# Deformable convolution: half blocks that share partitions, a map convolution read from SBUF, contraction in 32x32 tiles

## What is computed

```python
offset = conv2d(x, offset_w, offset_b)            # 3x3, 18 channels: (dy, dx) of 9 taps
mask = sigmoid(conv2d(x, mask_w, mask_b))         # 3x3, 9 channels
py = hs + ky + dy                                 # one sampling position per pixel and tap
px = ws + kx + dx
val = bilinear gather of x at (py, px), zero outside the image      # b k h w c
out = einsum('bkhwc,bkhw,ock->bohw', val, mask, weight)
x = x + out
```

## Time and profile before

| | us |
|---|---|
| median of 3 runs | 2114.85 |
| lowest and highest | 2094.2 and 2151.25 |
| profiled execution | 2127.27 |
| its span, first to last instruction | 2125.5 |
| PE busy | 1895.2 (89%) |
| DVE busy | 1278.3 (60%) |
| ACT busy | 1128.9 (53%) |
| POOL busy | 789.2 (37%) |

### The profile page before, as it was taken

The page is one execution under the profiler, slowest core; times in us unless marked ns, Lnnn a source line. Parts: engine busy times, 40 slices in busy tenths (PEclk is TensorE's granted clock), DMA queues, the critical chain, the costliest instruction groups (busy, mean ns, idle before and its releaser), DMA issues. The chain is left out here.

```text
span 2125.5 us, 58757 instructions
## 1 busy us (share of the span) xinstructions
PE 1895.2 (89%) x21269; PEld 1344.1 (63%) x21269; DVE 1278.3 (60%) x2688; ACT 1128.9 (53%) x3617; POOL 789.2 (37%) x743
## 2 busy tenths in 40 slices
PE   5599999999999998389999999596949999999998
PEld 3466666666666665145555556395827787778876
DVE  5178888888888888258878878642372222222222
ACT  2378888888888887357777778200211111111111
POOL 0077878878787876133323333000000011001100
PEclk9989999999999999589999999855879999999999
DMA  4400000000000000566666665240022111221110
GB/s 165 134 20 28 28 27 23 27 26 28 23 28 26 28 24 23 142 169 186 190 185 191 181 175 143 59 71 11 11 55 51 40 36 36 52 56 36 36 36 15
DMA packets 164173, 150.01 MB, mean 71 GB/s; under 512 B 60070, under 2 KB 151340, under 8 KB 163935
## 3 DMA queue, kind: packets, MB, share of 16 engines
q1 hardware_dynamic: 164014, 147.88, 26.2%
HBM read 83.18 MB, written 45.89 MB: 61 GB/s over the span
## 5 line engine op out<-in xcount | busy, mean ns | idle before, releaser
L412 ACT ACTIVATE at_probs<-at_sc,at_nmx 128x196 f32<-128x196 f32 x1152 | 473.0, 423 | 114.2 <-DVE at_nmx L358 114.2
L340 POOL TENSOR_TENSOR at_probs<-at_probs,at_rs 128x784 f32<-128x784 f32 x288 | 429.9, 1493 | 152.9 <-DVE at_rs L363 152.8
L358 DVE TENSOR_REDUCE at_nmx<-at_sc 128x4 f32<-128x784 f32 x288 | 277.4, 963 | 122.3 <-PE at_sc L436 122.3
L447 PE MATMUL at_pt<-at_ident,at_probs 128*98 128x128 f32 x2304 | 311.1, 278 | 40.6 <-DVE at_pts L368 40.0
L447 PEld LDWEIGHTS at_pt<-at_ident,at_probs 128*98 128x98 f32 x2304 | 241.1, 128 | 141.2 <-POOL at_probs L340 78.8
L436 PE MATMUL at_sc<-at_kw,at_qw 32*128 32x196 f32 x2304 | 272.1, 355 | 12.0 <-POOL at_qw L329 8.1
L1247 ACT ACTIVATE dn_mix<-dn_mps 128x432 f32<-128x432 f32 x384 | 182.3, 528 | 114.1 <-PE dn_mps L1142 110.6
L1930 POOL TENSOR_TENSOR fc_spo<-fc_prod 128x256 f32<-128x256 f32 x72 | 52.2, 725 | 502.6 <-DVE fc_prod L1974 502.6
L2031 PE MATMUL fc_qps<-fc_wk,fc_xs 99*128 99x128 f32 x1728 | 208.4, 278 | 31.3 <-DMA fc_xs<-in_ones 31.3
L412 ACT ACTIVATION_READ_ACCUMULATOR at_probs<-at_sc,at_nmx 128x1 f32 x1152 | 235.9, 205 | 0.0
L2031 PEld LDWEIGHTS fc_qps<-fc_wk,fc_xs 99*128 99x128 f32 x1728 | 202.0, 194 | 42.0 <-issue 39.1
(11 more groups left out here) (155 smaller groups left out, 2527.9 us busy)
## 6 DMA issues: line engine op xcount, KB each, us to landing
fc_xs<-fc_xp SPq DMA_DIRECT2D x144, 120.0 KB
dn_slab<-near_image SPq DMA_DIRECT2D x72, 200.0 KB, 4.2
at_vs<-attention_values SPq DMA_DIRECT2D x288, 49.0 KB
dn_offs<-near_maps SPq DMA_DIRECT2D x24, 486.0 KB
near_corners<-dn_split SPq DMA_DIRECT2D x24, 486.0 KB
dn_stack<-near_corners SPq DMA_DIRECT2D x24, 486.0 KB
dn_patch<-near_pixels SPq DMA_DIRECT2D x24, 384.0 KB
attention_values<-ap_vrow SPq DMA_DIRECT2D x21, 256.0 KB, 2.3
```

The lines of the kernel that those rows point to most:

```text
L340: nc.gpsimd.tensor_tensor(probs[s][p][:, :, :, :], probs[s][p][:, :, :, :], rs[s][:, 2 * p:2 * p + 2, :].unsqueeze(3).broadcast_to([P, 2, ...
L358: nc.vector.tensor_reduce(nmx[s][:, 2 * p:2 * p + 2, :], sc[p][:, :, 0:2 * NK].rearrange("p b (j k) -> p b j k", j=2), AX.X, ALU.max, nega ...
L412: nc.scalar.activation(probs[s][p][:, b, j, :], sc[p][:, b, NK * j:NK * j + NK], ACT.Exp, bias=nmx[s][:, 2 * p + b, j:j + 1], accum_out=su ...
L447: mm = nc.tensor.transpose(pt[b % 2][0:HK, o:o + P], probs[s][p][:, b % 2, j, HK * c:HK * c + HK], ident[:, :])
```

## The change

A block is now two half blocks of HBW = 4 columns each, 48 blocks of pixels being replaced by NBLK = 12 blocks of 8 columns. A half block reaches (4+4) x (4+4) = 64 pixels, so that the two halves lie in partitions 0 to 63 and 64 to 127 of `patch` and `mix`, and one column of the moving operand serves two output pixels. A step takes PER = 3 blocks; `mix` keeps its 432 columns, and a tile has 4 steps in place of 8. `stack` has 52 rows in place of 42 and its data rows come in two halves. `sample` is 24 matmuls of 64x32 tiles with 144 columns, one half block into each of two banks `sps[0]`, `sps[1]`, with images rotated by one column group in the second half.

The image in DRAM, `slab`, `store_image` and `load_slab` are gone: `conv` reads shifted views of a ring of 24 normalised rows in SBUF, as 72 matmuls of 32x32 tiles with 192 columns per tile of the image (18 units u of four), and writes the bank `cps`, which it now shares with `turn`. `contract` also becomes 72 matmuls of 32x32 tiles; units of the two alternate, one always on the diagonal tiles of the array while the other is on the tiles beside it. The maps are made five tiles ahead, `prepare` runs three ahead, and the order on SP, ACT, PE and DVE is written anew.

```diff
-DBW = 12
-DSTEPS = W // DBW
+HBW = 4
+DBW = 2 * HBW
+NBLK = W // DBW
+PER = 3
+DSTEPS = NBLK // PER
...
-PATCH = (DR + 4) * (DBW + 4)
+REACH = HBW + 4
+PATCH = 2 * (DR + 4) * REACH
...
-DATA = 18
+DATA = 36
+TAP_ORDER = (3, 4, 0, 1, 2, 6, 7, 8, 5)
...
             def load_maps(j):
                 sp.wait_ge(map_out, 16 * B * (j + 1))
                 if j >= 1:
-                    sp.wait_ge(corner_ready, 3 * j - 1)
-                sp.dma_start(offs[:, :, :].rearrange("p a n -> p (a n)"),
...
+                    sp.wait_ge(hats_ready, HATS * j - 1)
+                    sp.wait_ge(corner_ready, 3 * j - 2)
+                for h, c, b, n in ((0, 0, 0, B), (1, 1, 0, B - 1), (1, 0, B - 1, 1)):
+                    sp.dma_start(offs[3 * TAPS * b:3 * TAPS * (b + n), h, :, :].rearrange("p a n -> p (a n)"),
...
             def load_stack(j):
                 sp.wait_ge(corners_out, 16 * (j + 1))
+                if j >= 1:
+                    sp.wait_ge(stack_in, 32 * j)
                 if j >= 2:
                     sp.wait_ge(mix_done, B * DSTEPS * (j - 1))
-                sp.dma_start(stack[j % 2][0:DATA, :, :, :, :].rearrange("p b t m i -> p (b t) (m i)"),
-                             corner_d[j % 2, :, :].rearrange("(g r) (h n) -> (r h) g n", r=3, n=DPX)).then_inc(stack_in, 16)
+                for h in range(2):
+                    sp.dma_start(stack[j % 2][DATA // 2 * h:DATA // 2 * (h + 1), :, :, :, :].rearrange("p b t k n -> p (b t) (k n)"),
+                                 corner_d[j % 2, :, :].rearrange("(g r) (e n) -> (r e) g n", r=3, n=DPX)[:, :, DPX // 2 * h:DPX // 2 * (h + 1)]).then_inc(stack_in, 16)
...
             for t in range(DTILES):
                 if t + 1 < DTILES:
-                    store_corners(t + 1)
+                    load_stack(t + 1)
+                if t + 3 < DTILES:
+                    load_maps(t + 3)
+                if t + 1 < DTILES:
                     load_patch(t + 1)
-                if t + 3 < DTILES:
-                    store_maps(t + 3)
-                if t + 4 < DTILES:
-                    load_slab(t + 4)
-                if t + 1 < DTILES:
-                    load_stack(t + 1)
                 if t + 4 < DTILES:
                     store_pixels(t + 4)
-                if t + 6 < DTILES:
-                    store_image(t + 6)
                 save(t)
-                if t + 3 < DTILES:
-                    load_maps(t + 3)
+                if t + 4 < DTILES:
+                    store_maps(t + 4)
+                if t + 2 < DTILES:
+                    store_corners(t + 2)
...
+                side, n = PATCH // 2, TAPS * PX
+                for i in range(PER):
+                    for b in range(B):
+                        for h in range(2):
+                            c = (b + h) % B
+                            mm = nc.tensor.matmul(sps[h][C * c:C * c + C, n * i:n * i + n], patch[t % 2][side * h:side * h + side, PER * k + i, C * b:C * b + C],
+                                                  mix[s % 2][b][side * h:side * h + side, n * i:n * i + n], start=True, stop=True)
...
+            def contract(t, u):
+                h, tap = 1 - u // TAPS, u % TAPS
...
                     if s + 1 < NSTEP:
                         spread(s + 1)
-                    if k == 0 and t + 4 < DTILES:
-                        turn(t + 4)
-                    if t >= 1 and 1 <= k < 4:
-                        contract(t - 1, k - 1)
-                    if t + 4 < DTILES and k >= 5:
-                        conv(t + 4, k - 5)
+                    if k >= 1:
+                        for u in range(6 * k - 6, 6 * k):
+                            if t + 5 < DTILES:
+                                conv(t + 5, u)
+                            if t >= 1:
+                                contract(t - 1, u)
                     if t < DTILES:
                         sample(s)
+                    if k == 0 and t + 5 < DTILES:
+                        turn(t + 5)
...
+                    if k == 0 and t + 4 < DTILES:
+                        bias_maps(t + 4)
                     if s + 1 < NSTEP:
                         for b in (2, 3):
                             relu(s + 1, b)
-                    if t + 3 < DTILES and k == 0:
-                        bias_maps(t + 3)
-                    if t + 2 < DTILES and 1 <= k < 5:
-                        prepare(t + 2, k - 1)
-                    if t + 2 < DTILES and k == 6:
+                    if k == 0 and t + 2 < DTILES:
+                        prepare(t + 2, 3)
+                    if k >= 1 and t + 3 < DTILES:
+                        prepare(t + 3, k - 1)
+                    if k == 2 and t + 2 < DTILES:
                         high(t + 2)
```

More of the change, by code:

```diff
@@ L910, in _ @@
             sp.wait_ge(const_in, 16 * len(loads))
+        @block.gpsimd
+        def _(pool):
+            for tile in zeros:
+                nc.gpsimd.memset(tile, 0.0)
         @block.vector
@@ L1134, in spread @@
                 if k == 0:
[L1135 removed]
+                    pe.wait_ge(stack_in, 32 * (t + 1))
                 for b in range(B):
@@ L1158, in sample @@
-                mm.then_inc(sample_done, 1)
-            def contract(t, k):
-                if k == 0:
-                    pe.wait_ge(mix_dve, kept_count(DSTEPS * t + DSTEPS - 1))
-                    if t >= 1:
-                        pe.wait_ge(added, t)
-                for b in range(B):
-                    w, n = (k, 2 * b + k) if k < 2 else (2 + b, 8)
-                    mm = nc.tensor.matmul(ops[C * b:C * b + C, 0:DPX], wd[:, w, :], sampled[t % 2][:, n, :, :].rearrange("p m i -> p (m i)"),
-                                          start=(k == 0), stop=(k == 2))
-                if k == 2:
+                    pe.wait_ge(mix_dve, kept_count(s - 1, 1))
@@ L1173, in _ @@
             turn(1)
-            for kx in range(3):
-                conv(0, kx)
+            for u in range(2 * TAPS):
+                conv(0, u)
             turn(2)
-            for kx in range(3):
-                conv(1, kx)
+            for u in range(2 * TAPS):
+                conv(1, u)
             turn(3)
-            for kx in range(3):
-                conv(2, kx)
-            for kx in range(3):
-                conv(3, kx)
+            for j in (2, 3):
+                for u in range(2 * TAPS):
+                    conv(j, u)
+            turn(4)
+            for u in range(2 * TAPS):
+                conv(4, u)
             spread(0)
@@ L1261, in _ @@
             bias_maps(0)
+            prepare(0, 0)
             bias_maps(1)
-            for part in range(4):
+            for part in range(1, 4):
                 prepare(0, part)
+            bias_maps(2)
+            prepare(1, 0)
             high(0)
-            bias_maps(2)
-            for part in range(4):
+            for part in range(1, 4):
                 prepare(1, part)
+            bias_maps(3)
+            prepare(2, 0)
             high(1)
+            prepare(2, 1)
+            prepare(2, 2)
             for b in (2, 3):
@@ L1347, in residual @@
                 dve.wait_ge(saved, 16 * (t + 1))
[L1348 to L1349 removed]
+                for h in range(2):
+                    xv = x_sb[:, t * DPX:t * DPX + DPX].rearrange("p (r k h c) -> p h k r c", r=DR, k=NBLK, h=2)[:, h, :, :, :]
+                    half = ops[:, DPX // 2 * h:DPX // 2 * (h + 1)].rearrange("p (k r c) -> p k r c", k=NBLK, r=DR)
+                    nc.vector.tensor_tensor(xv, xv, half, ALU.add).then_inc(added, 1)
             for g in range(3):
@@ L1353, in _ @@
             keep_rows(1)
-            normalise(3)
-            normalise(4)
+            for g in range(3, 5):
+                normalise(g)
             keep_rows(2)
-            normalise(5)
             keep_rows(3)
-            largest(0)
-            largest(1)
-            largest(2)
+            for g in range(5, 7):
+                normalise(g)
+            for j in range(4):
+                largest(j)
+            keep_rows(4)
             for b in range(2):
@@ L1369, in _ @@
                             relu(s + 1, b)
-                    if k == 0 and t + 4 < DTILES:
-                        keep_rows(t + 4)
-                    if k == 1 and t + 6 < DTILES:
-                        normalise(t + 6)
-                    if k == 2 and t + 3 < DTILES:
-                        largest(t + 3)
-                    keep(s)
-                    if k == 4 and t >= 1:
+                    if k == 1 and t + 4 < DTILES:
+                        largest(t + 4)
+                    if k == 2 and t + 7 <= DTILES:
+                        normalise(t + 7)
+                    for h in range(2):
+                        keep(s, h)
+                    if k == 0 and t + 5 < DTILES:
+                        keep_rows(t + 5)
+                    if k == 3 and t >= 1:
                         residual(t - 1)
```

315 lines of the change are left out of this document (155 added, 160 removed).

## The result

The changed kernel takes 2190.16 us (median of 4 runs, 2180.44 to 2223.67) beside 2108.64 us for the kernel before (4 runs, 2094.2 to 2151.25). The ratio is 1.040, with a 95% interval from 1.030 to 1.049. Medians are over all runs; a ratio compares only the runs of each kernel that were not in the slower of the chip's two states. The profiled execution took 2194.76 us, with a span of 2192.9.

What follows compares the result with a forecast made beforehand. The loop of weights, 23.2 us per tile, was to bound the kernel: 923 + 23.5 + 464 (20 loops) + 60 ends the block at 1470.5, 109 us later, added to 2114.85 for 2224 us; range 2085 to 2290.

Steps and rivals of the forecast that it cites:

- the loop of weights: Making of weights once per tile through SP, ACT and POOL: A, B, C and D in sequence, 23.2 us.
- A: On ACT, from the landing of the maps to the end of `high`: 5.4 us.
- B: POOL's `rest`, 2.38 us, and a semaphore: 2.5 us.
- C: On SP, from `store_corners` issued to `load_stack` issued: taken as 3.9 us.
- D: From `load_stack` issued to maps landed: 11.4 us, the middle between 9.0 (bytes count) and 13.8 (packets count).
- the start: Block before the loops: third maps at 923, then one round of about 23.5 us to the fourth maps.
- the end: Block after the last tile's maps: 1.5 steps, three tiles of 13.5, last `contract` and `residual`, 60 us.
- On engines alone a tile would take 13.5 us: Engine work per tile in the block, PE's sum being 13.3 us; the launch would take about 2000 us.
- either fast loop: Rivals on the loop: no queueing in D, loop 17.1, 2091 us, chance 0.15; floor, loop 16.6, 2066 us, chance 0.12.
- A sum beside them: Claim that the engines' 2000 us would need B, C and D in 7 us.
- that rival: Clock rival: PE, idling some 7 us per tile, stays at 0.50, its 13.3 us becoming 27; 2300 us, chance 0.08.
- The four tiles of a unit that write one bank: Rival: `conv`'s 32x32 tiles take turns, `conv` 24 us and a tile 31.4; 2405 us, chance 0.05.

Runs made afterwards that it cites:

- no patch and one tap: Maps first, with patch loaded for the first two tiles alone and contract on its last tap alone (work left out): 2069.46 us, ratio to before 0.982.
- maps first: Changed kernel with load_maps(t + 3) moved ahead of load_stack(t + 1) in SP's round: 2168.32 us, ratio to before 1.022.

## Why the prediction was right

The forecast was 2224 us by one mechanism, the loop of weights. The mechanism holds: its four pieces follow one another in the timeline, ACT waits 9.9 us per tile where some 9 were forecast, and putting the maps ahead of the stack takes the wait away and the time down.

| term | forecast | measured |
|---|---|---|
| A | 5.4 | 5.0 |
| B | 2.5 | 2.5 |
| C | 3.9 | 3.7 |
| D | 11.4 (9.0 to 13.8) | 10.8 |
| loop | 23.2 | 22.0 |

The measured pieces are averages over 20 tiles.

**The block.** It was forecast to end at 1470.5. Its last instruction ended at 1454.2, and the stage began 8.9 us later than in the profile before, so 25 us are to be accounted for. The 20 loops were 24 us shorter, the start was 7 us shorter, and the end 6 us longer. The forecast's 109 us added to the block were 85 in the profiles (599.2 - 514.0); the medians are 81.5 apart.

**The mis-sized term** is D, and through it the loop. Its value was near by luck, its reason was not right. I took 11.4 as the middle between the stack load costing its bytes and costing its packets. The runs show bytes, or little more, for the stack. By bytes D was to be 9.0, and 9.0 it is, once the patch's loads no longer follow directly. The other 1.8 us come from the patch behind the maps, which my working left out. The rule of the Trainium skill for the number of engines ("DMA: Bandwidth & Descriptors", section "Why a DMA increments its semaphore by 16 and not by 1"), which I set at 13.8, decided nothing: 10.8 stood below it, and cutting the load at row 16 made D longer.

**The step that failed** is one that the result did not hang on: "On engines alone a tile would take 13.5 us". With the loop out of the way the floor is 16.1 us in PE's own list, from groups of 2.4 us for 2.0 and two waits for DVE, and on top come the issue gaps with their half clock. Had either fast loop been right (2091 or 2066), PE would most likely have set the time: the complete versions with the maps ahead of the stack and `conv` and `contract` interleaved, in which ACT hardly waits for maps, take 2126 to 2181 us. So the chance of 0.27 that I gave to those two rivals was on times that no complete version here reached, the best being 2126. A sum beside them was wrong too: with A at 5.4 a tile of 13.5 us leaves 8.1 for B, C and D, not 7.

**The other rivals.** The clock did fall, to 0.90 in the block, and in part as that rival had it, behind PE's waits for weights: of 16 stretches at 0.50 between 940 and 1340 us, eight follow a wait for ACT's `relu`s alone, five an issue gap alone, two both and one a wait for DVE. But it came back to 1.00 after 3.4 to 10.2 us each time, and the loop was the longer path. The 0.91 of "no patch and one tap" is one stretch of 92 us from 1257 on, in the last tiles, which have no `conv` left; from 940 until there its clock was 1.00. The four tiles of a unit that write one bank do run together: 24 matmuls of 192 columns take 2.39 us, where one after the other at 0.34 would take 8.2. By "TensorEngine Tiling (Array Packing)" of the Trainium skill, section "Restrictions and Gotchas", row tiles cannot access one bank at the same time; for tiles on different partitions of the bank this trace contradicts it.

## What to carry to other kernels

When a change halves the work of the busiest engine, list next what passes through single buffers and in-order queues once per iteration, and add it up as a loop: here the sum of four pieces came within 6% of the period. Count for a transfer's landing what is queued ahead and also what is issued while it runs. And before crediting engine work that is cut into many small matmuls, expect the instruction stream to take part: with the loop out of the way a tile of a complete version with interleaved matmuls took 18.5 to 21.3 us, depending on when the DMA traffic came, and 16.5 with work left out, not the 13.3 of the columns.

## What the runs showed of the hardware that was not expected

- PE stopped with no data wait 14 times in 400 us of the changed kernel, six times for 2.5 us or more. More traffic in one burst meant more of it: 43.0 us with maps first, 17.5 with the same work and bytes but the patch later, 20.1 with 768 KB less per tile, 0.8 with fewer instructions too. In 960 to 1320 us the changed kernel has 66 packets of instructions and the kernel before 63, at the higher mean DMA share of 0.67, so neither mean rate explains it. "Runtime: NRT & Kernel Launch" of the Trainium skill, section "Instruction fetch mechanics", says that instructions come in blocks over a DMA queue and that the cost at a block's end is mostly hidden. The traces agree: a queue of its own brings one packet of 16 KB for some 256 of PE's instructions, and 63 of 73 such packets in 400 us of the changed kernel have no gap over 1 us behind them.
- The traces tie the gaps to these packets. In the 14 kernels together PE has 110 issue gaps over 1 us between 940 and 1340 us, and each ended 1.2 to 2.4 us after such a packet had landed, 105 of them within 1.9; of 264 other waits of PE over 0.7 us only 22 ended 1.2 to 1.9 us behind one. In the gap of 4.71 us of "maps first" (1117.60 to 1122.31) the packet ran from 1119.72 to 1120.87; it is this row of the window 1118.5 to 1120 us (packets, MB, share of 16 engines), and the windows on either side have none:

```profile
q8 instruction: 1, 0.02, 4.8%
```

- These packets took 1.1 to 1.2 us on average before and after the change alike, so it is their start that came late. In the 2 us ahead of those with a gap behind them 13.1 data packets were under way on average in the changed kernel and 14.7 in "maps first", ahead of the others 9.0 and 9.4. That they were stuck behind data fits, but no trace shows when a packet was asked for, so this part is argued. What also stays open is why the kernel before, with its larger packets, hardly had gaps.
- Of the 15 times that PE stood idle for over 3 us in the changed kernel and in "maps first" (940 to 1340 us), whatever it waited for, 14 have a stretch at a clock of 0.50 that begins before or up to 1.2 us after the end and lasts 3.4 to 10.2 us. The gap of 4.71 us above so cost at least 1.9 us more: the `conv` and `contract` behind it took 4.3 us for 2.4.
- Cutting a transfer of 384 B packets in two at row 16 made it slower: share 1.38 at 120 GB/s against 0.82 at 149.
- The first 179 us of the stage behind the block ran at a clock of 0.64 in the profile of before and 0.76 in the changed kernel's, and the rest of the launch took 754.6 and 727.9 us. A difference of 27 us between two profiles can come from there alone:

```profile
1371.00:1550.00 179.00, 143.42 (x1075) 132.83 (x1076) 71.21 (x202) 26.38 (x48) 1.84 (x2) 0.64 0.19 35
```

```profile
1465.00:1644.00 179.00, 126.76 (x1112) 110.72 (x1112) 94.07 (x242) 31.18 (x62) 2.80 (x7) 0.76 0.20 40
```
